# Edge stage of a graph attention kernel: sums, weights and carry in one matmul stream, loops written out, membership in 32 bits

## Chip, cores and metric

One Trainium2 chip, one core. The metric is the device time in microseconds of one launch. All data are float32 except where bf16 is named.

## The reference, cut to what matters

There are 6250 nodes with 512 features, 8 heads of 64 features, and 100000 edges sorted by their destination `dst`.

```
h     = leaky_relu(layernorm(x) @ W.T + b)                 # N x 512
e     = leaky_relu(e_src[src] + e_dst[dst])                # E x 8, from h
a     = exp(e - m[dst]) / segment_sum(exp(...), dst) * dist
out   = segment_sum(h[src] * a, dst)                       # N x 512
x     = x + out
x     = x + ffn(layernorm(x))                              # small per-row network
```

## The kernel before

Four parts run one after the other. `project` makes h in 49 tiles of 128 nodes and stores rows of 520 numbers (512 values and the 8 source scores) in the HBM table `table_h`. `prepare` works out, for each group of edges, the first destination row (its base), the offsets `rel` from it, and a table `table_shifts` of destination scores in three bf16 parts. `attend_windows` (L647 to L955) is the edge stage, and `finish` (L958) divides by the weights, adds x and runs the network over 13 chunks.

The edge stage goes through 112 groups of 7 tiles of 128 edges. One group's destinations lie within a window of 128 rows. Per group:

- GpSimd issues 7 indirect DMAs (L768), each fetching 128 rows of `table_h`, 260 KB, into `gathered`, three slots deep. It waits for an index copy by ACT (`set_src`, L910) and for the messages of the group three before.
- The Vector engine writes the membership matrix in bf16 (L778: does edge p belong to row c). ACT widens it to 32 bits (`widen_member`, L928), TensorE transposes it in bf16 (L873), and ACT copies the transpose back (`turn_member`, L934).
- TensorE looks up the destination scores of each edge: 7 matmuls of 48 columns (`at_edges`, L864). The Vector engine sums the three parts (L786), makes the scores (L790 to L798), and ACT takes the exponentials (L920).
- ACT and the Vector engine split the exponentials into three bf16 parts. The Vector engine makes 7 messages of 512 columns (L810) from `gathered` into `msg`.
- TensorE sums the messages by membership: 7 matmuls 128x512 in float32 (L886, each issued as two instructions), and the weights by 7 bf16 matmuls of 24 columns (L893). ACT copies the sums out (`evacuate`), the Vector engine adds up the weights (L831).
- The last row of one window can be the first of the next. So SP stores a window to `table_agg` (L741), reads one row back for the next group (L752), and the Vector engine adds it (`carry_in`, L841), four rounds behind the front of the pipeline.

The order on each engine is written out by hand: each engine walks through rounds, and `stage(u, slot, lag, do)` lets it do the step `do` for group u - lag. The rounds are a loop of three at a time with register arithmetic (`rounds`, L703). On the Vector engine a round is: carry of u-4, scores of u-1, membership of u, messages of u-1, weights of u-3. On TensorE: lookup of u-1, first three tiles of u-2, transposes of u, the rest of u-2. Engines wait for one another by semaphores that count finished groups; SP's three DMAs of a round are issued in order: window of u, carry of u-4, store of u-4.

## Time and profile before

| what | value |
|---|---|
| time, median of 3 runs (lowest, highest) | 2029.5 us (2019.91 to 2036.35) |
| the profiled execution's own time | 2030.48 us |
| its span in the trace | 2028.7 us |
| TensorE matmul busy | 1406.5 us, 69% |
| Vector engine busy | 1337.0 us, 66% |
| GpSimd busy | 986.9 us, 49% |
| ACT busy | 496.3 us, 24% |
| DMA packets of the gathers | 208.78 MB, 37.1% of 16 engines' span |

The trace begins at the first instruction; starts are in microseconds from there. PE is TensorE's matmul unit, PEld its weight load, DVE the Vector engine, ACT ScalarE, POOL GpSimd, SP the engine that issues plain DMAs. A row's bracket holds the idle time of that engine just before it, and what ended that time; "remote" is a semaphore update for which the trace shows no instruction or DMA close enough in time.

### The profile page before, as it was taken

What the parts mean: (1) busy time and instruction counts of PE and PEld (TensorE: products, weight loads), DVE (VectorE), ACT (ScalarE), POOL (GpSimd) and SP (SyncE); (2) the same over time, 40 slices, a digit from 0 to 9 for tenths busy, and PEclk for the clock granted to TensorE, in tenths of its full rate; (3) what the DMA queues carried; (4) which work ended last, traced back from release to release, by engine and by line L of the source; (5) the groups of instructions that cost most, each with busy time, mean ns of one, the idle gap of its engine ahead of it and who ended that gap; (6) DMA issues with size and microseconds to landing.
All of it is one profiled execution on the core that took longest, in us unless ns stands there. A gap on an engine that the chain in (4) does not pass through costs nothing. (4 is left out here: it accounts for less than half of the span.)

```text
span 2028.7 us, 24635 instructions
## 1 busy us (share of the span) xinstructions
PE 1406.5 (69%) x5502; PEld 662.8 (33%) x5502; DVE 1337.0 (66%) x3092; ACT 496.3 (24%) x1141; POOL 986.9 (49%) x932
## 2 busy tenths in 40 slices
PE   5778783477666676566767676766657665299997
PEld 2333331233232233232323232323223332155555
DVE  5777776467566576665766576666657655868784
ACT  1222220222222222222322222222222221123332
POOL 1222221666656566575556755666666651213231
PEclk9999987688888898888888888888889878578888
DMA  5333333666665566575566765666666653424331
GB/s 216 131 124 126 125 125 64 166 195 191 176 175 172 169 191 191 168 200 168 160 172 194 199 171 159 191 178 174 172 188 182 188 165 91 176 89 167 145 135 67
DMA packets 151399, 326.44 MB, mean 161 GB/s; under 512 B 47312, under 2 KB 47568, under 8 KB 151246
## 3 DMA queue, kind: packets, MB, share of 16 engines
q0 software_dynamic: 62720, 208.78, 37.1%
q1 hardware_dynamic: 88654, 117.38, 17.2%
q8 instruction: 9, 0.15, 0.0%
q14 instruction: 16, 0.13, 0.0%
HBM read 255.82 MB, written 70.27 MB: 161 GB/s over the span
## 5 line engine op out<-in xcount | busy, mean ns | idle before, releaser
L768 POOL DMA_INDIRECT gathered<-table_h,w_src_idx x784 | 827.5, 1055 | 517.2 <-issue 244.3
L886 PE MATMUL bank<-w_msg,member 128*128 128x512 f32 x1568 | 810.3, 662 | 0.0
L810 DVE TENSOR_TENSOR w_msg<-gathered,w_coef 128x512 f32<-128x512 f32 x784 | 489.8, 694 | 3.9
L886 PEld LDWEIGHTS bank<-w_msg,member 128*128 128x128 f32 x1568 | 313.8, 213 | 316.3 <-issue 282.2
L873 PE MATMUL bank<-ident,member 128*128 128x128 bf16 x784 | 72.0, 240 | 313.8 <-DVE member L778 221.2
L786 DVE TENSOR_REDUCE at_dst<-bank 128x112 f32<-128x336 f32 x112 | 56.3, 503 | 326.8 <-remote 259.5
L277 PE MATMUL bank<-wt,xnT 128*128 128x512 f32 x392 | 203.0, 666 | 0.0
L208 POOL TENSOR_TENSOR prod_dst<-hrow,w_dst 128x512 f32<-128x512 f32 x49 | 75.6, 1543 | 250.4 <-DVE hrow L237 250.4
L920 ACT ACTIVATE w_ex<-w_diff 128x56 f32<-128x56 f32 x112 | 27.9, 249 | 673.2 <-issue 348.0
L873 PEld LDWEIGHTS bank<-ident,member 128*128 128x128 bf16 x784 | 53.5, 108 | 402.6 <-DVE member L778 221.4
L1197 PE MATMUL bank<-h,w 128*128 128x512 f32 (+1 forms) x338 | 180.3, 682 | 0.0
L841 DVE TENSOR_TENSOR summed<-summed,w_carry 1x520 f32<-1x520 f32 x111 | 76.4, 688 | 155.7 <-ACT summed L908 126.4
L1114 POOL TENSOR_TENSOR res<-x_in,y 128x2048 f32<-128x2048 f32 (+1 forms) x13 | 61.9, 4765 | 234.9 <-DMA out<-res 162.8
L908 ACT ACTIVATE memberT<-bank 128x896 bf16<-128x896 bf16 x112 | 102.1, 911 | 266.0 <-remote 239.3
L778 DVE TENSOR_TENSOR member<-node_no,k_rel 128x896 bf16<-128x896 f32 x112 | 122.1, 1090 | 9.6 <-DMA node_no<-in_node_no 9.6
L908 ACT ACTIVATE member<-member 128x896 f32<-128x896 bf16 x112 | 106.5, 951 | 64.0 <-issue 35.0
L864 PE MATMUL bank<-window,memberT 128*128 128x48 bf16 x784 | 40.3, 190 | 117.4 <-ACT memberT L908 94.8
L277 PEld LDWEIGHTS bank<-wt,xnT 128*128 128x128 f32 x392 | 78.0, 209 | 95.7 <-issue 95.7
L1197 PEld LDWEIGHTS bank<-h,w 128*128 128x128 f32 x338 | 68.8, 223 | 64.3 <-issue 62.3
L286 PE MATMUL bank<-ident,xn 128*128 128x128 f32 x196 | 32.3, 289 | 78.7 <-DVE xn L227 78.7
L1143 ACT ACTIVATE h<-bank,b 128x512 f32<-128x512 f32 (+1 forms) x65 | 41.7, 661 | 162.7 <-PE bank L1208 90.6
L1208 PEld LDWEIGHTS bank<-w,h 128*128 128x128 f32 x490 | 72.0, 225 | 21.7 <-issue 20.9
(133 smaller groups left out, 1185.8 us busy)
## 6 DMA issues: line engine op xcount, KB each, us to landing
table_agg<-summed SPq DMA_DIRECT2D x112, 260.0 KB
table_agg<-zeros SPq DMA_DIRECT2D x50, 260.0 KB, 2.2
table_h<-hrow SPq DMA_DIRECT2D x49, 260.0 KB, 2.1
xt<-in_x SPq DMA_DIRECT2D x49, 256.0 KB, 2.7
gathered<-table_h,w_src_idx POOLq DMA_INDIRECT x784
agg_in<-table_agg SPq DMA_DIRECT2D x12, 1040.0 KB, 7.7
x_in<-in_x SPq DMA_DIRECT2D x12, 1024.0 KB, 5.4
out<-res SPq DMA_DIRECT2D x12, 1024.0 KB, 4.4
```

The lines of the kernel that those rows point to most:

```text
L208: nc.gpsimd.tensor_tensor(prod_dst[:, s, :], hrow[:, s, 0:D], w_dst[:, :], ALU.mult).then_inc(s_pdst, 1)
L277: mm = nc.tensor.matmul(ps_h[s][:, :], xnT[:, s, c * P:(c + 1) * P], wt[:, c, :], start=False, stop=(c == DC - 1))
L768: pool.indirect_dma_start(out=gathered[:, s, j, :], out_offset=None, in_=t["h"][:, :], in_offset=bass.IndirectOffsetOnAxis(ap=src_idx[:, s ...
L778: nc.vector.tensor_tensor(member16[:, s, :, :], node_no[:, :].unsqueeze(1).to_broadcast([P, GROUP, P]), keep["rel"][:, bass.ds(g * GROUP, ...
L810: nc.vector.tensor_tensor(msg[:, s, j, :].rearrange("p (h d) -> p h d", h=HEADS), gathered[:, s, j, 0:D].rearrange("p (h d) -> p h d", h=H ...
L841: nc.vector.tensor_tensor(summed[0:1, s, :], summed[0:1, s, :], carry[:, :], ALU.add).then_inc(d["carried"], 1)
L873: last = nc.tensor.transpose(member_t[:, j * P:(j + 1) * P], member16[:, s, j, :], ident16[:, :])
L886: nc.tensor.matmul(sums[s][:, :], member[:, s, j, :], msg[:, s, j, :], start=first, stop=final)
L908: return nc.scalar.activation(out, in_, ACT.Copy)
L1114: nc.gpsimd.tensor_tensor(res[:, s, 0:k, :], x[:, s, 0:k, :], y[:, s, 0:k, :], ALU.add).then_inc(d["res"], 1)
L1197: last = nc.tensor.matmul(bank[:, 0:w], w2[:, weights, :], h1[:, units, 0:w], start=(i == 0), stop=(i == len(pairs) - 1))
L1208: last = nc.tensor.matmul(y3[:, 8 * j:8 * j + 8], h2[:, g, j * P:(j + 1) * P], w3[:, g, :], start=(g == 0), stop=(g == 4))
```

## The change

- A row of the tables is now two halves of 260: 256 values and 4 head scores or weights each. Helper functions give the views.
- A group holds 895 edges; the slot of row 32 of its first tile is kept free (`CARRY_ROW`), with offset 0. There are still 112 groups.
- The exponentials are written by ACT into `gathered` itself, beside the values; the messages overwrite the values in place. TensorE sums values and weights together in two matmuls of 260 columns per tile, into two PSUM banks. The separate bf16 weight matmuls, the splitting into parts and the weights' evacuation are gone.
- The carried row is no longer added by the Vector engine. SP reads it from `table_agg` into row 32 of the group's first tile (`carry_in`), and that tile is summed last (`add_rest`). A group's final matmuls thus wait until the group before has been summed, copied out, stored and read back.
- The Vector engine writes the membership in 32 bits; it is transposed in 32 bits over two PSUM banks, and ACT copies it to bf16. ACT's widening is gone.
- The coefficients and the row of node numbers lie in PSUM. The lookup stays in one PSUM bank.
- Four slots in place of three. All loops of the stage are written out, and GpSimd reads its indices from the resident array; ACT's index copy is gone. GpSimd waits for the sums of the group four before.
- DMA semaphores count 16 per transfer in place of 48.
- SP's order in a round: window of u+2, store of u-1, carry of u.

The other parts follow the new row layout. Left out below are removed lines of the edge stage and edits of the same kind elsewhere.

```diff
@@ -30,9 +30,12 @@
 ROWS = NODES + P
 NOWHERE = NODES
 DC = D // P
-ROW = D + HEADS
+HALF = D // 2 + HEADS // 2
+ROW = 2 * HALF
 GROUP = 7
-GROUPS = -(-E // (P * GROUP))
+CARRY_ROW = 32
+GROUP_EDGES = P * GROUP - 1
+GROUPS = -(-E // GROUP_EDGES)
 EDGE_TILES = GROUPS * GROUP
 TINY = 1e-30
 FAR = 1 << 20
@@ -54,6 +57,42 @@
+def row_values(rows):
+    return rows.rearrange("p (a w) -> p a w", a=2)[:, :, 0:D // 2].rearrange("p a (h d) -> p a h d", d=HD)
+def row_heads(rows):
+    return rows.rearrange("p (a w) -> p a w", a=2)[:, :, D // 2:HALF]
+def rows_heads(rows):
+    return rows.rearrange("p k (a w) -> p k a w", a=2)[:, :, :, D // 2:HALF]
+def by_half(heads):
+    return heads.rearrange("p (a h) -> p a h", a=2)
+def tiles_by_half(heads):
+    return heads.rearrange("p k (a h) -> p k a h", a=2)
+def wide(values):
+    return values.rearrange("p (a h d) -> p a h d", a=2, d=HD)
...
                 dve.wait_ge(d["dstf"], 1)
                 step(nc.vector.tensor_tensor(rel, rel, keep["bases"][:, :].unsqueeze(2)
                                                     .to_broadcast(group_dst), ALU.subtract))
+                step(nc.vector.memset(rel[CARRY_ROW:CARRY_ROW + 1, :, 0], 0.0))
                 nc.vector.tensor_reduce(spread[:, 0:GROUPS], rel, AX, ALU.max).then_inc(d["rel_max"], 1)
...
-def attend_windows(nc, top, banks, t, keep, branch_semaphores):
...
+def attend_windows(nc, top, psum, t, keep, branch_semaphores):
     with ExitStack() as ctx:
         def sb(name, shape, dt=F32):
@@ -659,300 +693,237 @@
             return branch_semaphores.pop() if branch_semaphores else top.enter_context(nc.semaphore(name))
...
+        S = 4
+        PARTS = 6 * HEADS
+        gathered = sb("gathered", [P, S, GROUP, ROW])
+        member = sb("member", [P, S, GROUP, P])
+        memberT = sb("memberT", [P, S, GROUP, P], BF16)
+        window = sb("window", [P, S, PARTS], BF16)
         at_dst = sb("at_dst", [P, GROUP, 2 * HEADS])
         score = sb("w_score", [P, GROUP, HEADS])
         leaky = sb("w_leaky", [P, GROUP, HEADS])
...
+        diff = sb("w_diff", [P, S, GROUP, HEADS])
+        summed = sb("summed", [P, S, ROW])
+        node_sb = sb("node_no", [P, P])
+        member_t = psum[:, 4:6, :].rearrange("p b c -> p (b c)")
+        coef = psum[:, 6, 0:GROUP * HEADS]
+        node_no = psum[:, 6, GROUP * HEADS:GROUP * HEADS + P]
+        s_no, s_no_kept = sem("node_no_loaded"), sem("node_no_kept")
         s_pool_on = sem("w_pool_went_on")
...
+        s_g = [sem(f"w_gathered{i}") for i in range(S)]
+        s_put = [sem(f"w_stored{i}") for i in range(S)]
+        s_carry = sem("w_carry_put")
+        s_win = [sem(f"w_window_loaded{i}") for i in range(S)]
+        names = ("member member_t memberT edge_dst at_dst score leaky diff ex coef msg sums evac").split()
         d = {k: sem("w_" + k) for k in names}
...
+        def filled(g, per):
+            return per * (g // S + 1)
+        def sums_of(slot):
+            return psum[:, 2 * (slot % 2):2 * (slot % 2) + 2, 0:HALF]
+        def edge_dst(slot):
+            return psum[:, 7, 0:GROUP * PARTS]
+        def rounds(lead, drain):
+            for u in range(-lead, GROUPS + drain):
+                yield u, u % S
         def stage(u, slot, lag, do):
...
+            if not 0 <= u - lag < GROUPS:
                 return
...
+            do(u - lag, (slot - lag) % S)
+        def old(g, slots=S):
+            return g >= slots
         with nc.Block() as block:
             @block.sync
             def _(sp):
...
+                sp.dma_start(node_sb[:, :], t["node_no"]).then_inc(s_no, 16)
+                def base_of(g):
+                    return sp.value_load(keep["bases_int"][0:1, g:g + 1], min_val=0, max_val=NODES)
                 def load_window(g, s):
...
+                    base = base_of(g)
                     if old(g):
...
+                        sp.wait_ge(d["edge_dst"], g - S + 1)
+                    sp.dma_start(window[:, s, :], t["shifts"][bass.ds(base, P), :]).then_inc(s_win[s], 16)
                 def store(g, s):
...
+                    base = base_of(g)
+                    if old(g, 1):
+                        before = (s - 1) % S
+                        sp.wait_ge(s_put[before], filled(g - 1, 16))
+                    sp.wait_ge(d["evac"], g + 1)
+                    sp.dma_start(t["agg"][bass.ds(base, P), :], summed[:, s, :]).then_inc(s_put[s], 16)
+                def carry_in(g, s):
+                    to = gathered[CARRY_ROW:CARRY_ROW + 1, s, 0, :]
+                    if not old(g, 1):
+                        sp.wait_ge(d["msg"], 1)
+                        sp.dma_start(to, t["h"][NODES:NODES + 1, :]).then_inc(s_carry, 16)
                         return
...
+                    base = base_of(g)
+                    before = (s - 1) % S
+                    sp.wait_ge(s_put[before], filled(g - 1, 16))
+                    sp.wait_ge(d["msg"], g * GROUP + 1)
+                    sp.dma_start(to, t["agg"][bass.ds(base, 1), :]).then_inc(s_carry, 16)
+                for u, slot in rounds(2, 1):
+                    stage(u, slot, -2, load_window)
+                    stage(u, slot, 1, store)
+                    stage(u, slot, 0, carry_in)
+                for g in range(GROUPS - S, GROUPS):
+                    sp.wait_ge(s_put[g % S], filled(g, 16))
             @block.gpsimd
             def _(pool):
...
+                for g in range(GROUPS):
+                    s = g % S
                     if old(g):
...
+                        wait_alone(pool, d["sums"], g - S + 1, s_pool_on)
                     for j in range(GROUP):
                         pool.indirect_dma_start(
                             out=gathered[:, s, j, :], out_offset=None, in_=t["h"][:, :],
...
+                            in_offset=bass.IndirectOffsetOnAxis(ap=keep["src"][:, g, j:j + 1], axis=0)
+                        ).then_inc(s_g[s], 16)
             @block.vector
             def _(dve):
                 def make_member(g, s):
                     if old(g):
...
+                        dve.wait_ge(d["sums"], g - S + 1)
                     nc.vector.tensor_tensor(
...
+                        member[:, s, :, :], node_no.unsqueeze(1).to_broadcast([P, GROUP, P]),
+                        keep["rel"][:, g * GROUP:(g + 1) * GROUP].unsqueeze(2).to_broadcast([P, GROUP, P]),
+                        ALU.is_equal).then_inc(d["member"], 1)
                 def scores(g, s):
...
                     dve.wait_ge(d["edge_dst"], g + 1)
                     nc.vector.tensor_reduce(
...
+                        at_dst[:, :, :], edge_dst(s).rearrange("p (j q c) -> p j c q", j=GROUP, q=3), AX, ALU.add
+                    ).then_inc(d["at_dst"], 1)
                     dve.wait_ge(d["at_dst"], g + 1)
...
+                    dve.wait_ge(s_g[s], filled(g, 16 * GROUP))
+                    nc.vector.tensor_tensor(tiles_by_half(score[:, :, :]), rows_heads(gathered[:, s, :, :]),
+                                            tiles_by_half(at_dst[:, :, 0:HEADS]), ALU.add).then_inc(d["score"], 1)
                     dve.wait_ge(d["score"], g + 1)
                     nc.vector.scalar_tensor_tensor(leaky[:, :, :], score[:, :, :], SLOPE, score[:, :, :], ALU.mult,
                                                    ALU.max).then_inc(d["leaky"], 1)
                     dve.wait_ge(d["leaky"], g + 1)
                     if old(g):
...
+                        dve.wait_ge(d["ex"], g - S + 1)
                     nc.vector.tensor_tensor(diff[:, s, :, :], leaky[:, :, :], at_dst[:, :, HEADS:], ALU.subtract
                                             ).then_inc(d["diff"], 1)
                 def messages(g, s):
                     dve.wait_ge(d["ex"], g + 1)
...
+                    nc.vector.tensor_tensor(
+                        tiles_by_half(coef.rearrange("p (j h) -> p j h", j=GROUP)), rows_heads(gathered[:, s, :, :]),
+                        tiles_by_half(keep["dist"][:, g * GROUP:(g + 1) * GROUP, :]), ALU.mult
+                    ).then_inc(d["coef"], 1)
                     dve.wait_ge(d["coef"], g + 1)
...
                     for j in range(GROUP):
+                        values = row_values(gathered[:, s, j, :])
                         nc.vector.tensor_tensor(
...
+                            values, values, by_half(coef[:, j * HEADS:(j + 1) * HEADS]).unsqueeze(3)
+                            .to_broadcast([P, 2, HEADS // 2, HD]), ALU.mult).then_inc(d["msg"], 1)
                 dve.wait_ge(s_no, 16)
...
+                nc.vector.tensor_copy(node_no, node_sb[:, :]).then_inc(s_no_kept, 1)
+                dve.wait_ge(s_no_kept, 1)
+                for u, slot in rounds(1, 0):
+                    stage(u, slot, 0, scores)
+                    stage(u, slot, -1, make_member)
+                    stage(u, slot, 0, messages)
             @block.tensor
             def _(pe):
+                def transpose(g, s):
+                    pe.wait_ge(d["member"], g + 1)
+                    if old(g, 1):
+                        pe.wait_ge(d["memberT"], g)
+                    for j in range(GROUP):
+                        last = nc.tensor.transpose(member_t[:, j * P:(j + 1) * P], member[:, s, j, :],
+                                                   keep["ident"][:, :])
+                    last.then_inc(d["member_t"], 1)
                 def at_edges(g, s):
...
                     pe.wait_ge(d["memberT"], g + 1)
...
+                    pe.wait_ge(s_win[s], filled(g, 16))
+                    if old(g, 1):
                         pe.wait_ge(d["at_dst"], g)
                     for j in range(GROUP):
...
+                        last = nc.tensor.matmul(edge_dst(s)[:, j * PARTS:(j + 1) * PARTS], memberT[:, s, j, :],
                                                 window[:, s, :], start=True, stop=True)
                     last.then_inc(d["edge_dst"], 1)
...
+                def add_tile(g, s, j, start, stop):
+                    for a in range(2):
+                        last = nc.tensor.matmul(sums_of(s)[:, a, :], member[:, s, j, :],
+                                                gathered[:, s, j, a * HALF:(a + 1) * HALF], start=start, stop=stop)
+                    return last
+                def add_first(g, s):
+                    pe.wait_ge(d["member"], g + 1)
+                    if old(g, 2):
+                        pe.wait_ge(d["evac"], g - 1)
+                    for j in range(1, 5):
                         pe.wait_ge(d["msg"], g * GROUP + j + 1)
...
+                        add_tile(g, s, j, j == 1, False)
+                def add_rest(g, s):
+                    for j in range(5, GROUP):
+                        pe.wait_ge(d["msg"], g * GROUP + j + 1)
+                        add_tile(g, s, j, False, False)
+                    pe.wait_ge(s_carry, 16 * (g + 1))
+                    add_tile(g, s, 0, False, True).then_inc(d["sums"], 1)
+                for u, slot in rounds(1, 0):
+                    stage(u, slot, -1, transpose)
+                    stage(u, slot, 0, add_first)
+                    stage(u, slot, -1, at_edges)
+                    stage(u, slot, 0, add_rest)
             @block.scalar
             def _(act):
                 def copy(out, in_):
                     return nc.scalar.activation(out, in_, ACT.Copy)
...
                 def exps(g, s):
                     act.wait_ge(d["diff"], g + 1)
...
+                    nc.scalar.activation(rows_heads(gathered[:, s, :, :]), tiles_by_half(diff[:, s, :, :]), ACT.Exp
+                                         ).then_inc(d["ex"], 1)
                 def turn_member(g, s):
                     act.wait_ge(d["member_t"], g + 1)
                     if old(g):
...
+                        act.wait_ge(d["edge_dst"], g - S + 1)
                     copy(memberT[:, s, :, :], member_t[:, 0:GROUP * P].rearrange("p (j c) -> p j c", j=GROUP)
                          ).then_inc(d["memberT"], 1)
                 def evacuate(g, s):
                     act.wait_ge(d["sums"], g + 1)
                     if old(g):
...
+                        act.wait_ge(s_put[s], filled(g - S, 16))
+                    copy(summed[:, s, :].rearrange("p (a w) -> p a w", a=2), sums_of(s)).then_inc(d["evac"], 1)
+                for u, slot in rounds(1, 1):
+                    stage(u, slot, 0, exps)
+                    stage(u, slot, 1, evacuate)
+                    stage(u, slot, -1, turn_member)
...
-                    nc.vector.tensor_scalar_max(wsum[:, 0:k, :], ak[:, :, D:ROW], TINY).then_inc(d["wsum"], 1)
+                    nc.vector.tensor_scalar_max(tiles_by_half(wsum[:, 0:k, :]), rows_heads(ak), TINY).then_inc(d["wsum"], 1)
...
-        banks = [top.enter_context(nc.psum_tensor(f"bank{i}", [P, 512], F32)) for i in range(8)]
+        psum = top.enter_context(nc.psum_tensor("bank", [P, 8, 512], F32))
+        banks = [psum[:, i, :] for i in range(8)]
...
+    edge_slots = np.delete(np.arange(GROUP * P), CARRY_ROW)
     for name, ends in (("src", src), ("dst", dst)):
-        padded = np.full(EDGE_TILES * P, NOWHERE, np.int32)
+        padded = np.full(GROUPS * GROUP_EDGES, NOWHERE, np.int32)
         padded[:E] = ends
-        a[name] = padded.reshape(GROUPS, GROUP, P).transpose(2, 0, 1)
+        slots = np.full((GROUPS, GROUP * P), NOWHERE, np.int32)
+        slots[:, edge_slots] = padded.reshape(GROUPS, GROUP_EDGES)
+        a[name] = slots.reshape(GROUPS, GROUP, P).transpose(2, 0, 1)
```

## Rows read from the trace of the kernel before

**Rows 1.** Windows: length; busy PE, PEld, DVE, ACT, POOL; PEclk, DMA share, GB/s
```profile
356.00:1724.00 1368.00, 902.70 (x3920) 412.37 (x3920) 862.32 (x1903) 343.30 (x783) 827.45 (x784) 0.85 0.62 176
1724.00:2028.70 304.70, 258.39 (x945) 145.79 (x945) 223.00 (x706) 82.16 (x158) 81.56 (x91) 0.79 0.36 130
```

**Rows 2.** Line L768: ns least/median/greatest, first and last start
```profile
L768 POOL DMA_INDIRECT gathered<-table_h,w_src_idx x784: 940/946/1869, 356.8 to 1683.6; - x196
```

**Rows 3.** Groups by line, 356:1724: busy, mean ns | idle before, its end
```profile
L768 POOL DMA_INDIRECT gathered<-table_h,w_src_idx x784 | 827.5, 1055 | 517.2 <-issue 244.3 <-DVE w_msg L810 149.0 <-ACT w_src_idx L908 123.9
L886 PE MATMUL bank<-w_msg,member 128*128 128x512 f32 x1568 | 810.3, 662 | 0.0
L810 DVE TENSOR_TENSOR w_msg<-gathered,w_coef 128x512 f32<-128x512 f32 x784 | 489.8, 694 | 3.9
...
L908 ACT ACTIVATE member<-member 128x896 f32<-128x896 bf16 x112 | 106.5, 951 | 64.0 <-issue 35.0 <-DVE member L778 29.0
L841 DVE TENSOR_TENSOR summed<-summed,w_carry 1x520 f32<-1x520 f32 x111 | 76.4, 688 | 155.7 <-ACT summed L908 126.4 <-issue 11.6 <-DVE summed L831 10.0
...
L908 ACT ACTIVATE summed<-bank 128x512 f32<-128x512 f32 x112 | 66.2, 591 | 10.0 <-PE bank L893 10.0
L786 DVE TENSOR_REDUCE at_dst<-bank 128x112 f32<-128x336 f32 x112 | 56.3, 503 | 326.8 <-remote 259.5 <-PE bank L864 55.6 <-DMA gathered<-table_h,w_src_idx 11.6
```

**Rows 4.** Timeline from 909 us, a short round: start, duration, engine, line
```profile
909.83 0.51 DVE L786 TENSOR_REDUCE at_dst<-bank 128x112 f32<-128x336 f32 x1 [7.18 <-remote]
...
911.00 1.08 DVE L778 TENSOR_TENSOR member<-node_no,k_rel 128x896 bf16<-128x896 f32 x1
911.28 1.63 POOL L768 DMA_INDIRECT gathered<-table_h,w_src_idx  x1 [0.30 <-issue]
...
912.38 4.30 DVE L810 TENSOR_TENSOR w_msg<-gathered,w_coef 128x512 f32<-128x512 f32 x7
```

**Rows 5.** Timeline 918 to 947 us: a lookup's end and who waits for it
```profile
918.18 0.51 DVE L786 TENSOR_REDUCE at_dst<-bank 128x112 f32<-128x336 f32 x1 [0.32 <-PE bank L864]
...
926.18 0.34 PE L864 MATMUL bank<-window,memberT 128*128 128x48 bf16 x7 [0.38 <-issue]
...
934.47 0.95 POOL L768 DMA_INDIRECT gathered<-table_h,w_src_idx  x1 [0.30 <-issue]
938.37 0.51 DVE L786 TENSOR_REDUCE at_dst<-bank 128x112 f32<-128x336 f32 x1 [10.04 <-remote]
...
946.13 1.10 POOL L768 DMA_INDIRECT gathered<-table_h,w_src_idx  x1 [10.72 <-DVE w_msg L810]
```

**Rows 6.** Groups by line, `project`: a Vector operation with one PSUM input
```profile
L237 DVE TENSOR_TENSOR hrow<-leak,bank 128x512 f32<-128x512 f32 x43 | 29.4, 683 | 22.3 <-ACT leak L305 21.2
```

**Rows 7.** Timeline of PE: summing, and 32-bit transposes of `project`
```profile
152.53 0.65 PE L286 MATMUL bank<-ident,xn 128*128 128x128 f32 x4 [0.99 <-DVE xn L227]
...
1700.43 6.25 PE L886 MATMUL bank<-w_msg,member 128*128 128x512 f32 x14
```

**Rows 8.** The same pair after the last gather, 1713 to 1719 us
```profile
1713.48 0.42 SPq L741 DMA_DIRECT2D table_agg<-summed  x1
1715.76 0.28 SPq L752 DMA_DIRECT2D w_carry<-table_agg  x1
1717.21 0.69 DVE L841 TENSOR_TENSOR summed<-summed,w_carry 1x520 f32<-1x520 f32 x1 [2.87 <-DMA w_carry<-table_agg]
1718.07 0.42 SPq L741 DMA_DIRECT2D table_agg<-summed  x1
```

**Rows 9.** SP's stores and carry loads while gathers run, 902 to 928 us
```profile
902.83 0.43 SPq L741 DMA_DIRECT2D table_agg<-summed  x1
...
907.09 0.56 SPq L752 DMA_DIRECT2D w_carry<-table_agg  x1
918.03 0.42 SPq L741 DMA_DIRECT2D table_agg<-summed  x1
...
927.51 0.70 SPq L752 DMA_DIRECT2D w_carry<-table_agg  x1
```

251 lines of the change are left out of this document (32 added, 219 removed).

## The prediction

> **What bounds the kernel now.** I read the windows of the parts first. The edge stage takes 1368.0 of the span of 2028.7 us [rows 1], and in it no engine is busy all the time: TensorE 66%, the Vector engine 63%, GpSimd 60%, DMA at a share of 0.62. `finish` is left as it is but for views. So the question is what a round of the edge stage waits for. The first and the last of the 784 gathers start at 356.8 and 1683.6 us [rows 2], which makes a round of 7 gathers 7 x 1326.8 / 783 = 11.86 us, and 1368 - 112 x 11.86 = 40 us for the last group's way through.
>
> Next the groups by line [rows 3]. GpSimd spends a median of 946 ns on a gather [rows 2], and 0.30 us stand ahead of each one, also where it waits for nothing [rows 4, 5]: 1.25 us, or 8.75 us a round. Its waits beyond that are named: 149.0 us for messages and 123.9 us for the index copy. GpSimd is held back, so it is not the bound. The Vector engine waits 326.8 us ahead of the sum of the looked-up parts (L786), and 155.7 us ahead of the carry (L841).
>
> The timeline shows how. A short round is 918.18 - 909.83 = 8.35 us from one L786 to the next [rows 4, 5]; the Vector engine is then almost never idle. In the long round that follows, the lookup's matmuls are over at 926.5 us, and the Vector engine starts on them only at 938.37 us [rows 5], 11.9 us later, released by something that the view calls remote. GpSimd was issuing gathers all that time, the last at 934.47; then it stood until 946.13, since its slots were full. I read this as TensorE's announcement arriving late while gathers run. It is the reading that my number rests on most: 326.8 / 112 = 2.92 us a round. And 8.35 + 2.92 = 11.27, with 0.6 left to 11.86 for carry and order.
>
> **The change, part by part.** *Short round, Vector engine.* Gone are the carry add (688 ns [rows 3]), two splits (about 0.2 us each) and the weights' sum (about 0.2 us). Messages stay at 7, each with one input in PSUM now; such an operation of 512 columns takes 683 ns in `project` [rows 6], against 694 [rows 3], so no change. The membership in 32 bits: 896 columns in 1.08 us with bf16 out [rows 4]. 32 bits out can't be shorter than that by much (a 1x pass, as 896 columns against the messages' 512 show) and could cost more; I bound it by 1.08 and twice that, and take 1.1, since the rows with 32-bit output have the same time per column. That leaves about 7.1 us a round.
>
> *Short round, TensorE.* Seven tiles of 512 columns take 6.25 us [rows 7]; 520 columns in two matmuls instead of one are 6.25 x 520/512 = 6.35, if a weight load stays hidden behind 260 columns. If it doesn't, the bound is twice as many loads of 213 ns, their mean, beside matmuls: 14 x 0.2 = 2.8 us more. I take the first, as a 512 column matmul repeats every 0.43 us and a load is half of it. Transposes in 32 bits: four take 0.65 us in `project` [rows 7], seven about 1.0, where bf16 takes 0.93 at the low clock. The lookup is 0.34 us [rows 5], the weight matmuls (about 0.33 us) go. Together 7.7 us a round, a little more than before. In sequence: first message over 3.24 us after L786 (2.55 to its start, then 0.69 [rows 4]), tile 1 a message later at 3.85, four tiles of 0.91 us until 7.5, lookup until 7.8, next L786 at 7.9. A short round is 7.9 us, set by TensorE instead of the Vector engine.
>
> *GpSimd.* A gather beside a busy Vector engine is stretched, to 1.63 us at 911.28 us under the membership [rows 4], while it is 0.95 in the idle stretch [rows 5]. The mean is 1055 ns against a median of 946: 784 x 0.109 = 85 us. Node numbers and coefficients in PSUM may take this away. It is worth nothing as long as GpSimd waits for slots, and is kept for a rival below. The index copy's 123.9 us go too, and what is late next is the free slot. That is now given by the sums of four groups ago instead of the messages of three; sums trail messages by some 4 us, so GpSimd gains about half a round of lead.
>
> The Trainium skill, page SBUF — State Buffer, section Who interferes with whom, says that a Vector instruction with two SBUF inputs blocks GpSimd's reads only, and infers that descriptor generation isn't held up by it. By that the PSUM placing gives nothing and the 85 us stay; the stretched gather at 911.28 speaks against it.
>
> *ACT.* Its widening (951 ns), two small copies and the index copy go, the evacuation grows by 8 columns. ACT is busy a quarter of the stage; zero either way, covered by waits.
>
> *Late announcements.* Three a round come from TensorE, as before: transposes, lookup, sums. I keep 2.92 us a round; below it lies zero, above it twice the value, as the sums' announcement is now inside the carry's loop.
>
> *The carry's loop.* Before, it ran four rounds behind. Now each group's last matmuls wait for it, and behind them in TensorE's queue stand the next group's transposes, tiles and lookup. One turn of the loop: store issue to carry landed, then the last tile (0.91 plus 0.2 us), the copy out (591 ns [rows 3]) and 0.2 us of hand-overs, so 1.9 us. Without gathers, store to carry is 1717.21 - 1713.48 = 3.73 us [rows 8]. With gathers it is 907.09 - 902.83 = 4.26 to the issue [rows 9], and 1.45 to land [rows 8], so 5.7; in the slow stretch 9.48 + 1.45 = 10.9 [rows 9], where SP itself was slow. The turn is 5.6, 7.6 or 12.8 us. At 7.6 it is hidden under a round of 10.8; 0.1 us a round is what I put on it, from the 12.8 us turns that fall together with long rounds anyway.
>
> *The rest.* One more Vector step in `prepare`, below 1 us. Loops written out: the register work between instructions goes, which no row puts on a path; nothing.
>
> *Sum.* 7.9 + 2.9 + 0.1 = 10.9 us a round; 112 x 10.9 + 40 = 1261 us against 1368, so 107 us less. The profiled execution took 2030.5 us (span 2028.7), 1 us over the median of 2029.5. That gives 1923, rounded to 1920 us.
>
> **The rivals.**
> *A. GpSimd's rate becomes the bound.* If late announcements go away with this rewrite (the fourth slot, increments of 16, fewer engines waiting), a round is 8.75 us: 1020 us for the stage, a time of about 1680. With the stretched gathers it is 7 x 1.355 = 9.49, and 1770. For it: GpSimd was the next in line by 2 us a round. Against: nothing in the diff touches the gathers' traffic, beside which lateness appears. Chance 0.21.
> *B. Announcements come only when the gathers pause.* After the last gather at 934.47 + 0.95 the lookup was taken up 2.95 us later [rows 5]. If a round always needs such a pause, it is 8.75 + 2.95 = 11.7 us whatever the other engines save: 1351 us, about 2013, within 1%. With smaller variations of other terms, chance 0.13.
> *C. The carry's loop stops TensorE; slower.* Place: the wait for the carry ahead of the last tile. Price: the middle of the 7.6 and 12.8 us turns, 10.2, plus one late announcement of 2.92 that the loop now holds, makes 13.1 us a round; 1508 us, a time of 2170. It decides from 11.86 us a turn up. For it: SP needed 9.5 us from store to carry load in a stretch with gathers [rows 9], and GpSimd will run gathers more of the time. Against: the short turn of 7.6 leaves 3 us. Chance 0.26, mostly between 2050 and 2180.
> That the change doesn't do what it says I take as no case: the operations are plainly other ones.
>
> **How the numbers follow.** The forecast's own case, 1790 to 2005 us (short rounds of 7.9 to 8.7 with 2 to 3 us of lateness), has 0.40. About 1% is what a measurement of this kernel can tell from no change, 20 us. Faster by over 1%: 0.40 + 0.21 = 0.61. Within: 0.13. Slower: 0.26. The range goes from 1690, which leaves out 0.07 below (A without a rest), to 2130, which leaves out about 0.11 of C.
>
> **What would show it.** Right: the mean distance of two gather groups falls from 11.86 to about 10.9 us; L786's counterpart still waits for "remote" or TensorE some 300 us in all; the Vector engine's share falls below 60%; matmuls of 260 columns repeat every 0.22 us. A shows as gathers 1.25 us apart without gaps and a mean of 0.95 us. B shows as a pause of about 3 us after each 7 or 14 gathers. C shows as TensorE idle ahead of its last tile, released by the carry's DMA, and gathers held by sums. Wrong in size would be weight loads that no longer hide (matmuls of 260 columns over 0.3 us apart), and a membership of 2 us.

## The result, and the profile after

The changed kernel takes 1934.7 us (median of 4 runs, 1919.3 to 1954.7) where the kernel before takes 2024.7; the ratio is 0.956, 95% interval 0.945 to 0.967. The forecast was 1920 us. Medians are of all executions, ratios of those in which the chip was not slowed by a lower granted clock, so a ratio can differ from the quotient of two medians. The profiled execution took 1919.3 us with a span of 1917.7, 110.9 us less than the span before.

Windows of the kernel after (columns as in [rows 1]): first the edge stage, then everything from TensorE's first instruction of `finish` on.

```profile
356.00:1635.00 1279.00, 943.29 (x4704) 756.06 (x4704) 736.42 (x1457) 191.09 (x337) 741.21 (x784) 0.89 0.66 189
1665.60:1917.70 252.10, 234.65 (x945) 133.68 (x945) 200.54 (x658) 80.60 (x155) 77.88 (x85) 0.90 0.37 136
```

The same second window before, from its own first instruction of `finish`:

```profile
1753.10:2028.70 275.60, 258.39 (x945) 145.75 (x945) 200.49 (x658) 80.36 (x155) 76.10 (x86) 0.82 0.34 125
```

So 23.5 of the 110.9 us are hardly the change's: `finish` has the same matmuls, and TensorE was busy in it for 23.7 us less at a granted clock of 0.90 instead of 0.82. The stretch from first to last gather went from 1326.8 us [rows 2] to 1248.0 (next row), 78.8 less. The last 8.6 us lie between the two.

The gathers' line after (as [rows 2]), and the groups by line of 356 to 1635 us (as [rows 3]):

```profile
L797 POOL DMA_INDIRECT gathered<-table_h,k_src x784: 940/946/1297, 356.7 to 1604.7; - x196
```

```profile
L875 PE MATMUL bank<-gathered,member 128*128 128x260 f32 x3136 | 817.6, 416 | 61.8 <-DVE gathered L839 39.8 <-issue 14.0 <-DMA gathered<-table_agg 7.7
L797 POOL DMA_INDIRECT gathered<-table_h,k_src x784 | 741.2, 945 | 524.8 <-issue 237.0 <-PE bank L875 169.6 <-remote 118.2
...
L839 DVE TENSOR_TENSOR gathered<-gathered,bank 128x512 f32<-128x512 f32 x784 | 478.7, 683 | 3.8
...
L807 DVE TENSOR_TENSOR member<-bank,k_rel 128x896 f32<-128x896 f32 x112 | 121.4, 1084 | 0.1
...
L903 ACT ACTIVATE summed<-bank 128x520 f32<-128x520 f32 x112 | 66.5, 594 | 71.8 <-remote 45.0 <-PE bank L875 14.8 <-issue 12.0
L814 DVE TENSOR_REDUCE at_dst<-bank 128x112 f32<-128x336 f32 x112 | 56.9, 508 | 510.9 <-remote 401.3 <-PE bank L868 108.5 <-issue 1.1
```

A round is 7 x 1248.0 / 783 = 11.16 us, where 10.9 was forecast. One gather of 784 takes over 1 us, 1297 ns, where 228 did before (mean 945 ns, before 1055). The Vector engine is busy 736 of 1279 us (58%), and nearly all its idle time stands ahead of L814, which answers to L786: 511 us, 4.56 a round.

The timeline of a regular round after:

```profile
904.26 0.94 POOL L797 DMA_INDIRECT gathered<-table_h,k_src  x1 [4.13 <-PE bank L875]
...
909.20 0.34 PE L868 MATMUL bank<-window,memberT 128*128 128x48 bf16 x7
...
909.38 2.88 PE L875 MATMUL bank<-gathered,member 128*128 128x260 f32 x12
...
911.76 0.95 POOL L797 DMA_INDIRECT gathered<-table_h,k_src  x1 [0.30 <-issue]
912.84 0.51 DVE L814 TENSOR_REDUCE at_dst<-bank 128x112 f32<-128x336 f32 x1 [4.38 <-remote]
...
914.35 0.60 ACT L903 ACTIVATE summed<-bank 128x520 f32<-128x520 f32 x1
...
915.13 0.94 POOL L797 DMA_INDIRECT gathered<-table_h,k_src  x1 [2.42 <-remote]
915.15 0.75 PEld L858 LDWEIGHTS bank<-ident,member 128*128 128x128 f32 x7 [3.31 <-DVE member L807]
915.15 0.98 PE L858 MATMUL bank<-ident,member 128*128 128x128 f32 x7 [2.90 <-DVE member L807]
915.17 0.35 SPq L769 DMA_DIRECT2D table_agg<-summed  x1
```

Seven gathers run from 904.26 to 912.71. The lookup is over at 909.54, and the Vector engine takes it up at 912.84, 0.13 us after the last gather's end. The sums are over at 912.26; ACT takes them at 914.35, and GpSimd starts the next run at 915.13. That is rival B's picture: a run of 8.45 us, a pause of 2.4 us, in which the announcements arrive. Set against the trace's record of every semaphore, it holds widely. Of 112 lookups 92 end inside a run; 96 are announced over 0.3 us late, and 88 of those 96 only outside a run. Early in a run it is different: 61 of the 112 announcements of transposes fall due 1 to 3 us into one, and their median delay is 0.01 us, while 52 lookups fall due 5 to 7 us into one and are 3.0 us late on average. Only TensorE's announcements are late. Those on record of the Vector engine's and ACT's once-a-round operations in this stage all come within 0.5 us of the operation's end (median 0.01), in both kernels.

### The profile page after: what moved, and what is told of

Same layout as the page of the kernel before. It is cut to its first block and busy times, and to the rows that moved or that the text cites. A ratio compares the mean times of both kernels' runs of the same rounds, so it can differ in the third digit from the quotient of the medians.

```text
span 1917.7 us, 22261 instructions
## 1 busy us (share of the span) xinstructions
PE 1422.5 (74%) x6286; PEld 994.0 (52%) x6286; DVE 1211.4 (63%) x2647; ACT 343.9 (18%) x692; POOL 902.5 (47%) x932
## 5 line engine op out<-in xcount | busy, mean ns | idle before, releaser
L797 POOL DMA_INDIRECT gathered<-table_h,k_src x784 | 741.2, 945 | 524.8 <-issue 237.0
L875 PE MATMUL bank<-gathered,member 128*128 128x260 f32 x3136 | 817.6, 416 | 61.8 <-DVE gathered L839 39.8
L875 PEld LDWEIGHTS bank<-gathered,member 128*128 128x128 f32 x3136 | 627.7, 207 | 188.2 <-issue 79.4
L839 DVE TENSOR_TENSOR gathered<-gathered,bank 128x512 f32<-128x512 f32 x784 | 478.7, 683 | 3.8
L814 DVE TENSOR_REDUCE at_dst<-bank 128x112 f32<-128x336 f32 x112 | 56.9, 508 | 510.9 <-remote 401.3
L858 PE MATMUL bank<-ident,member 128*128 128x128 f32 x784 | 130.4, 315 | 290.4 <-DVE member L807 274.1
L858 PEld LDWEIGHTS bank<-ident,member 128*128 128x128 f32 x784 | 100.7, 160 | 333.0 <-DVE member L807 313.6
L903 ACT ACTIVATE memberT<-bank 128x896 bf16<-128x896 f32 x112 | 102.6, 916 | 181.4 <-PE bank L858 108.6
L807 DVE TENSOR_TENSOR member<-bank,k_rel 128x896 f32<-128x896 f32 x112 | 121.4, 1084 | 0.1
L903 ACT ACTIVATE summed<-bank 128x520 f32<-128x520 f32 x112 | 66.5, 594 | 71.8 <-remote 45.0
L1179 PE MATMUL bank<-w,h 128*128 128x8 f32 x490 | 62.6, 262 | 0.5 <-ACT h L1114 0.5
```

What stands on the lines that cost most here:

```text
L797: pool.indirect_dma_start(out=gathered[:, s, j, :], out_offset=None, in_=t["h"][:, :], in_offset=bass.IndirectOffsetOnAxis(ap=keep["src"][ ...
L807: nc.vector.tensor_tensor(member[:, s, :, :], node_no.unsqueeze(1).to_broadcast([P, GROUP, P]), keep["rel"][:, g * GROUP:(g + 1) * GROUP]. ...
L814: nc.vector.tensor_reduce(at_dst[:, :, :], edge_dst(s).rearrange("p (j q c) -> p j c q", j=GROUP, q=3), AX, ALU.add).then_inc(d["at_dst"], 1)
L839: nc.vector.tensor_tensor(values, values, by_half(coef[:, j * HEADS:(j + 1) * HEADS]).unsqueeze(3) .to_broadcast([P, 2, HEADS // 2, HD]), ...
L858: last = nc.tensor.transpose(member_t[:, j * P:(j + 1) * P], member[:, s, j, :], keep["ident"][:, :])
L875: last = nc.tensor.matmul(sums_of(s)[:, a, :], member[:, s, j, :], gathered[:, s, j, a * HALF:(a + 1) * HALF], start=start, stop=stop)
```

## The experiments

Each ratio is to the kernel before, timed beside the experiment on the same chip. Experiments 1 to 4, 5 to 8, 9 to 11 and 12 ran on four chips, and the kernel after was not timed again on them. So its 0.956 is compared across chips, and small differences to it prove little.

Two theories were put against each other. S is the sum of the prediction: work of a short round plus late announcements. L (later L2) says that an unbroken run of gathers holds back what TensorE announces, until the run ends. To compare kernels I split each round into the gathers, 7 x (mean + 0.30 us), and the rest, in which GpSimd stands. Before that is 9.48 + 2.38 = 11.86 us [rows 2, 3], after 8.72 + 2.44 = 11.16.

**1. After, with the PSUM placing undone.**

```diff
-        coef = psum[:, 6, 0:GROUP * HEADS]
-        node_no = psum[:, 6, GROUP * HEADS:GROUP * HEADS + P]
+        coef = sb("w_coef", [P, GROUP * HEADS])[:, :]
+        node_no = sb("node_no_kept", [P, P])[:, :]
```

> The changed kernel with coefficients and node numbers back in SBUF, nothing else. Theory L (a round is one run of 7 gathers plus a pause of 2.4 us, because TensorE's announcements that fall due inside a run come only at its end): the gathers are stretched again, mean 1.05 instead of 0.945 us, so a run is 0.77 us longer and the time rises by 112 x 0.77 = 86 us, to about 2020 us; the gain over the kernel before is gone. Theory S (the prediction's sum: a round is TensorE's short round of 7.9 us plus 2.9 us of late announcements, and GpSimd waits for slots anyway): the gathers are stretched, but the time stays at 1935 us within 1%.

1891.6 us, ratio to before 0.948 (0.939 to 0.958). Its gathers' line, and two groups by line:

```profile
L797 POOL DMA_INDIRECT gathered<-table_h,k_src x784: 940/946/1897, 358.8 to 1576.3; - x196
```

```profile
L797 POOL DMA_INDIRECT gathered<-table_h,k_src x784 | 793.4, 1012 | 442.1 <-issue 241.2 <-PE bank L875 103.1 <-remote 97.8
...
L814 DVE TENSOR_REDUCE at_dst<-bank 128x112 f32<-128x336 f32 x112 | 56.9, 508 | 467.8 <-remote 334.4 <-PE bank L868 108.8 <-issue 24.7
```

The gathers are stretched again, and the time does not rise: 9.18 + 1.70 = 10.88 us a round. Theory L as written falls here. Against this run the kernel after has shorter gathers (8.72) and longer pauses (2.44), so the placing brought nothing that can be seen. The hold is weaker here: 29 lookups fall due 5 to 7 us into a run, and half of them are announced within 0.02 us, where the median of the 52 in the kernel after is 3.1 us.

**2. Before, with that placing alone.**

```diff
-        node_no = sb("node_no", [P, P])
+        node_sb = sb("node_no", [P, P])
+        node_no = banks[5][:, 0:P]
...
-        coef = sb("w_coef", [P, GROUP, HEADS])
+        coef = banks[7][:, 0:GROUP * HEADS].rearrange("p (j h) -> p j h", j=GROUP)
```

> The kernel before, with only its coefficients and node numbers put in two free PSUM banks. Theory L: the gathers' mean falls from 1.055 to 0.945 us, and the time by up to 86 us, to 1940 to 1960 us, with nothing else of the rewrite done. Theory S: gathers shorter, time 2025 us within 1%, as the round is set by the Vector engine's work plus late announcements.

2163.6 us, ratio 1.088 (1.077 to 1.099): slower, which neither theory expected. Its gathers' line and the timeline of one lookup:

```profile
L769 POOL DMA_INDIRECT gathered<-table_h,w_src_idx x784: 942/949/1337, 356.0 to 1832.9; - x196
```

```profile
935.10 0.33 PE L867 MATMUL bank<-window,memberT 128*128 128x48 bf16 x7
...
944.45 0.94 POOL L769 DMA_INDIRECT gathered<-table_h,w_src_idx  x1 [0.30 <-issue]
947.98 0.51 DVE L787 TENSOR_REDUCE at_dst<-bank 128x112 f32<-128x336 f32 x1 [12.24 <-remote]
...
955.63 1.11 POOL L769 DMA_INDIRECT gathered<-table_h,w_src_idx  x1 [10.24 <-DVE w_msg L811]
```

A round is 8.81 + 4.39 = 13.20 us. Here 14 gathers run without a break, 0.95 us each, and the lookup that was over at 935.43 is taken up 12.6 us later, 2.6 us after the run's end. The hold is as long as what is left of the run. The unbroken runs got no longer on average: counting gathers under 0.4 us apart as one run, there are 79 runs of 9.9 gathers, where the kernel before has 58 of 13.5. What rose is the lookups' mean delay, from 2.6 to 4.9 us. Where Vector operations stretch the gathers, announcements do get through inside a run (experiment 1). That this is why taking the stretching away costs more than it brings is argued from the two runs, not shown.

**3. After, with the lookup a round ahead.**

```diff
-                for u, slot in rounds(1, 0):
-                    stage(u, slot, -1, transpose)
+                for u, slot in rounds(2, 0):
+                    stage(u, slot, -1, at_edges)
+                    stage(u, slot, -2, transpose)
                     stage(u, slot, 0, add_first)
-                    stage(u, slot, -1, at_edges)
                     stage(u, slot, 0, add_rest)
```

(The membership and ACT's copy of it move a round ahead likewise.)

> The changed kernel with membership, transposes and lookup one round further ahead: the lookup of group g+1 stands at the head of TensorE's round g instead of in its middle, so its announcement has a whole round to arrive. Theory L: the Vector engine no longer stands at the end of each run; its idle time ahead of the sum of looked-up parts falls from 511 us to under 150, and the round becomes the gathers' own 8.75 us if TensorE's sums can be announced late without stopping GpSimd: 1935 - 112 x 2.2 = 1690 us; if each run still needs its pause for the sums, 1900 to 1935. Theory S: TensorE's own sequence stays, lateness leaves the path: 7.9 to 8.75 us a round, the same 1690. A rival H, that lateness is TensorE being behind its modelled times and not held announcements: no change, 1935 us.

1865.0 us, ratio 0.937 (0.926 to 0.948, which overlaps after's interval at its edge); 8.72 + 1.89 = 10.61 us a round. Timeline and group by line:

```profile
910.41 0.34 PE L868 MATMUL bank<-window,memberT 128*128 128x48 bf16 x7
910.59 0.96 PE L858 MATMUL bank<-ident,member 128*128 128x128 f32 x7
911.39 5.21 PE L875 MATMUL bank<-gathered,member 128*128 128x260 f32 x23
...
921.12 0.95 POOL L797 DMA_INDIRECT gathered<-table_h,k_src  x1 [0.30 <-issue]
...
924.66 0.92 ACT L903 ACTIVATE memberT<-bank 128x896 bf16<-128x896 f32 x1 [12.12 <-remote]
```

```profile
L903 ACT ACTIVATE memberT<-bank 128x896 bf16<-128x896 f32 x112 | 102.6, 916 | 482.4 <-remote 373.5 <-PE bank L858 84.9 <-issue 24.0
...
L814 DVE TENSOR_REDUCE at_dst<-bank 128x112 f32<-128x336 f32 x112 | 56.2, 502 | 219.2 <-remote 205.1 <-PE bank L868 8.8 <-issue 5.4
```

The Vector engine's wait fell by 292 us, but the round by only 0.55: the expected 1690 us failed. The lateness moved to the transposes. They are over at 911.55, ACT gets them at 924.66, 2.6 us after a run of 14 gathers ends, and in ACT's queue the exponentials stand behind them. TensorE itself went on with its sums at 911.39, so its work was not late, only its word.

**4. After, with an eighth of the bytes.**

```diff
-                            out=gathered[:, s, j, :], out_offset=None, in_=t["h"][:, :],
+                            out=gathered[:, s, j, :] if g < S else gathered[:, s, j, 0:65], out_offset=None,
+                            in_=t["h"][:, :] if g < S else t["h"].rearrange("r (b c) -> (r b) c", b=8),
```

> The changed kernel with gathers that bring 65 columns (260 bytes) a row instead of 520, from the fifth group on; it leaves out the rest of each row and reads other rows, the number of gathers and descriptors stays. If announcements are held by GpSimd issuing gathers: runs of 8.5 us remain, announcements still come at their ends, time 1935 us within 1.5%. If they are held by the gathers' traffic: the Vector engine's idle time ahead of the sum of looked-up parts goes from 511 to under 150 us, the round falls to 8 to 8.8 us and the time to 1610 to 1700 us.

1908.7 us (one run), beside 2000.3 for the kernel before on the same chip; the window of its edge stage and its gathers' line:

```profile
356.00:1600.00 1244.00, 926.15 (x4696) 745.31 (x4697) 736.03 (x1457) 191.34 (x336) 740.19 (x784) 0.90 0.23 52
```

```profile
L797 POOL DMA_INDIRECT gathered<-table_h,k_src x784: 938/944/1297, 355.9 to 1577.1; - x196
```

DMA moves 52 GB/s instead of 189, and a round is still 8.71 + 2.21 = 10.92 us. So the bytes moved are not what holds the announcements. What is left is GpSimd's issuing itself, or the DMA queue's handling of the row requests, whose number this run keeps; no run separates the two.

**5. After, with GpSimd waiting for the lookup ahead of its 5th gather.**

```diff
                     for j in range(GROUP):
+                        if old(g) and j == 4:
+                            wait_alone(pool, d["edge_dst"], g - 1, s_pool_on)
```

> The changed kernel with one more wait in GpSimd's queue: ahead of the 5th of its 7 gathers it waits for the lookup that TensorE does meanwhile, so that a run is cut where that announcement falls due. Theory L2 (GpSimd's issuing holds back what TensorE announces later than some 3 us into an unbroken run, until the run ends): the lookup's announcement comes within 1 us of its end, the Vector engine's idle time ahead of the sum of looked-up parts falls from 511 to under 250 us, and the round from 11.1 to 9 to 9.8 us: 1700 to 1800 us. Rival T (lateness belongs to TensorE's own queue, or to the number of gathers under way, and not to the unbroken run): the added wait only delays gathers; no change or slower, 1935 to 2050 us.

1882.9 us, ratio 0.945 (0.938 to 0.953): far from the 1700 to 1800 expected. The timeline:

```profile
910.76 0.95 POOL L799 DMA_INDIRECT gathered<-table_h,k_src  x1 [0.30 <-issue]
910.99 0.34 PE L870 MATMUL bank<-window,memberT 128*128 128x48 bf16 x7
...
913.17 0.51 DVE L816 TENSOR_REDUCE at_dst<-bank 128x112 f32<-128x336 f32 x1 [3.98 <-remote]
...
913.94 0.94 POOL L799 DMA_INDIRECT gathered<-table_h,k_src  x1 [2.24 <-remote]
```

The run was not cut, it was shifted: of 109 restarts after a pause 108 now stand ahead of a 5th gather, and 106 of 111 runs are still 7 gathers long. Each lookup is announced 1.5 us after a run's end (median), and none of the 105 late ones inside a run. So the hold follows the run wherever the run is put, which speaks for L2 and against T. L2's price was wrong, since a pause costs 2.3 us each time.

**6. Experiment 3 with a wait for the transposes ahead of the 4th gather.**

```diff
+                        if old(g) and j == 3:
+                            wait_alone(pool, d["member_t"], g, s_pool_on)
```

> The version with membership, transposes and lookup a round ahead, and a wait ahead of GpSimd's 4th gather of a group for the transposes that TensorE does meanwhile. Theory L2: a long run can no longer form while TensorE owes an announcement; the transposes' late announcements (ACT idle 373 us by remote) go below 100 us, the round falls from 10.6 to 8.9 to 9.5 us, 1865 us to 1660 to 1740. Rival T: as the added wait costs GpSimd time, 1865 us or more.

1845.3 us, ratio 0.927 (0.919 to 0.935); 8.72 + 1.78 = 10.50 us a round. The ratio is lower than in experiment 3, but the intervals overlap. The size expected by L2 failed: 40 pauses stand ahead of a first gather and 34 ahead of a 4th, so one kind of pause took the place of another.

**7. After, with the 32-bit membership undone** (Vector engine writes bf16, TensorE transposes bf16, ACT widens):

```diff
-                        member[:, s, :, :], node_no.unsqueeze(1).to_broadcast([P, GROUP, P]),
+                        member16[:, s, :, :], node_no.unsqueeze(1).to_broadcast([P, GROUP, P]),
...
+                    copy(member[:, s, :, :], member16[:, s, :, :]).then_inc(d["member"], 1)
```

> The changed kernel with the membership part undone: written in bf16 by the Vector engine, transposed in bf16 by TensorE, widened to 32 bits by ACT. Theory S and theory L2 alike: ACT's 0.95 us a round beside the transposes is covered, transposes cost 0.9 to 1.0 us either way: 1915 to 1950 us, no change. A rival for it (32 bits on the Vector engine save a hand-over from ACT on the path): slower by 112 x 0.5 to 1 us, 1990 to 2050 us.

1920.0 us, ratio 0.962 (0.954 to 0.970), where after has 0.956: no difference that can be told. The part that names the change brought nothing.

**8. Before, with its loop written out and no index copy.**

```diff
-                    wait_alone(pool, s_idx, g + 1, s_pool_on)
...
-                            in_offset=bass.IndirectOffsetOnAxis(ap=src_idx[:, s, j:j + 1], axis=0)
+                            in_offset=bass.IndirectOffsetOnAxis(ap=keep["src"][:, g, j:j + 1], axis=0)
```

> The kernel before with its edge stage's loop written out and the gathers' indices read where they lie, so without ACT's index copy and GpSimd's 124 us of waits for it; nothing else of the rewrite. Theory S (GpSimd is held back by slots anyway; register work is on no path): 2025 us within 1%. Theory L2: GpSimd waits for messages instead, at longer unbroken runs, so announcements are no earlier: 2025 to 2100 us. Rival R (the gain came with the written-out loops and the missing index copy): 1920 to 1960 us.

2087.3 us against 1988.5, ratio 1.039 (1.026 to 1.052). Three things changed at once: the loops, ACT's index copy and GpSimd's wait of 124 us for it. Together they made the kernel slower. So rival R falls, and letting GpSimd run on did not help, as in experiment 2. Which of the three costs the time was not tried.

**9 and 10. Both kernels with gathers in their first groups alone.**

> The changed kernel with gathers for its first 4 groups alone; later groups compute on what then lies in the slots, so its outputs are not the reference's. It measures a round without gathers. Theory S as written in the prediction: the short round is 7.9 us, set by TensorE. Theory L2 the same, and all idle time of the Vector engine ahead of the sum of looked-up parts that is called remote (401 us) goes, since nothing is issued that could hold an announcement: stage of about 900 us, time of about 1555 us. If TensorE's lateness were its own (its matmuls really taking longer than modelled), the round would stay at 10 to 11 us.

> The kernel before with gathers for its first 3 groups alone; later groups compute on what then lies in the slots, so its outputs are not the reference's. Its short round by the prediction is 8.35 us: 112 x 8.35 = 935 us for the stage, time of about 1620 us. By theory L2 no lookup is announced late any more (the Vector engine's 260 us by remote go). The difference to the changed kernel without gathers is what the rewrite saved in work and order: 0.45 us a round if theory S's terms hold.

1557.8 and 1579.8 us (one run each). The line of the looked-up sums, after and then before, and after's group by line:

```profile
L814 DVE TENSOR_REDUCE at_dst<-bank x112: 507/507/508, 358.8 to 1255.1; 128x112 f32<-128x336 f32 x112
```

```profile
L786 DVE TENSOR_REDUCE at_dst<-bank x112: 487/489/509, 368.8 to 1262.9; 128x112 f32<-128x336 f32 x112
```

```profile
L814 DVE TENSOR_REDUCE at_dst<-bank 128x112 f32<-128x336 f32 x112 | 56.8, 507 | 149.0 <-PE bank L868 127.4 <-remote 21.6
```

First to last, that is 896.3 / 111 = 8.07 us a round after and 894.1 / 111 = 8.05 before. But these means hold the start. The second and third of these sums, after and then before:

```profile
393.80 0.51 DVE L814 TENSOR_REDUCE at_dst<-bank 128x112 f32<-128x336 f32 x1 [21.60 <-remote]
403.25 0.51 DVE L814 TENSOR_REDUCE at_dst<-bank 128x112 f32<-128x336 f32 x1 [2.74 <-PE bank L868]
```

```profile
380.48 0.51 DVE L786 TENSOR_REDUCE at_dst<-bank 128x112 f32<-128x336 f32 x1 [4.58 <-issue]
389.37 0.51 DVE L786 TENSOR_REDUCE at_dst<-bank 128x112 f32<-128x336 f32 x1 [1.90 <-PE bank L864]
```

The kernel after issues its first 28 gathers in one run, also here, and its second lookup is taken up only behind it, 35.0 us after the first; before, that step is 11.7 us. From the third sum to the last a steady round is (1255.1 - 403.25) / 109 = 7.82 us after and (1262.9 - 389.37) / 109 = 8.01 before. Two things follow. The 401 us of "remote" are gone but for that one wait of 21.6 us, so all lateness comes with the gathers. And the rewrite's saved operations are worth 0.19 us a round by themselves, which the slower start eats up here. Of the 22 us between the two times, 10 lie ahead of the first lookup (358.8 against 368.8) and 8 in `finish`.

The Trainium skill, page Perfetto Trace Analysis, section Summary: the profiler window per engine type, says that TensorE's end in the profile is estimated and the propagation of its semaphore hidden, so that lateness could be work still going on. Here it isn't: with no gathers the same matmuls are announced on time, and in experiment 3 TensorE's next matmuls are recorded while the word is still out.

**11. Experiment 3 with the PSUM placing undone.**

> The version with membership, transposes and lookup a round ahead, with coefficients and node numbers back in SBUF. Theory L2 with what e1_sbuf showed (gathers stretched under Vector operations with two SBUF inputs let announcements through inside a run): the gathers cost 0.4 us a round more, the pauses 0.7 us less: ratio to before 0.925 to 0.935, where the same version with them in PSUM had 0.937. Theory S: nothing, 0.937. A rival (stretched gathers add to a round that they set now): 0.955.

1846.0 us, ratio 0.9215 (0.914 to 0.929): faster than the kernel before, and its interval lies below after's, which was measured on another chip. A round is 9.25 + 1.29 = 10.54 us.

```profile
L797 POOL DMA_INDIRECT gathered<-table_h,k_src x784: 940/946/1867, 355.8 to 1534.7; - x196
```

As L2 expected, gathers are 0.5 us a round longer than in experiment 3 and pauses 0.6 shorter.

**12. Lookup ahead, GpSimd's wait of experiment 6 and no PSUM placing, together.**

> The version a round ahead with coefficients and node numbers in SBUF, and GpSimd's wait ahead of the 4th gather of a group for TensorE's transposes. Theory L2, if the two effects add: runs of 14 gathers (43 of 58 in e11_ahead_sbuf) are cut, ACT's idle time by remote ahead of the turned membership goes from 223 to under 120 us: ratio to before 0.905 to 0.918. A rival (each cut run costs its own pause of 2.3 us, and that eats what earlier announcements bring): 0.92 to 0.93.

1723.2 us, ratio 0.957 (0.952 to 0.961). This ran on another chip. There the kernel before took 1803.9 us, where it had taken 1988.5 to 2024.7 elsewhere, and its granted clock was 0.93 where it had been 0.86. The ratio can't be set beside the others, and the question of the run stays open. Its gathers' line and the longest waits:

```profile
L799 POOL DMA_INDIRECT gathered<-table_h,k_src x784: 942/947/2066, 358.3 to 1410.0; - x196
```

```profile
DVE w_score L821 <- DMA gathered<-table_h,k_src: 307.6, 112, 7.6
POOL gathered L799 <- issue: 253.1, 776, 16.8
```

On that chip all 784 gathers run without a pause, 7 x 1051.7 / 783 = 9.40 us a round, and the 224 announcements of transposes and sums arrive within 0.02 us of their ends. Rival A, which put 9.49 us on a round of stretched gathers, is what bounds it. No other kernel was traced on this chip, so the trace does not tell whether the chip or the kernel's version ended the hold; that the kernel before gained 10% there too speaks for the chip.

## Why the prediction was right

**The time.** 1920 forecast, 1934.7 measured; by profiled executions 1923 and 1919.3, helped by 23.5 us in `finish`, at a higher clock, that I had not put in. In the stage alone 107 us were forecast and 87 came (78.8 + 8.6). So the close hit is in part luck.

**Terms that held.** Membership in 32 bits 1084 ns (1.1 us put), messages 683, seven transposes 0.98 us (1.0), copy out 594, the Vector engine's share 58% (below 60%). From L814 to the lookup's end it was 7.78 us at the full clock (923.74 to 931.52), with 7.8 put. Matmuls of 260 columns repeat every 2.88 / 12 = 0.24 us (0.22 put), weight loads stay hidden. The clock was my gap: in the round from 912.84 us that stretch was 9.16 us long, and 16 matmuls in it took 5.13 us instead of 3.75. The windows of those matmuls show a granted clock of 0.73, a mean of both levels, and of 1.00:

```profile
916.70:921.80 5.10, 5.10 (x22) 4.14 (x23) 2.84 (x5) 0.39 (x1) 3.88 (x5) 0.73 0.77 210
927.60:931.30 3.70, 3.70 (x21) 3.14 (x22) 2.85 (x5) 0.40 (x1) 2.78 (x4) 1.00 0.75 197
```


**Late announcements.** I kept this term as it was, and by the lookups' own delay it stayed: 2.61 us on average from end to announcement before, 2.75 after. The 2.92 that I wrote was another measure, all idle time ahead of the sum of looked-up parts, with 67 us of waits for TensorE and DMA in it. By that measure the term grew to 4.56 us a round, and the sign of "some 300 us in all" came out at 511, 401 of them remote against 259.5 [rows 3]: the Vector engine has less to do (busy 736 us, before 862 [rows 1]) and waits the longer. Nor is the delay a constant that a rewrite leaves alone, as I treated it. It is what is left of a run when the word falls due: 3.3 us in after's regular round, 11.9 us before [rows 5], 12.6 in experiment 2. Rival B named that mechanism, at 0.13, and its sign is there: 92 of 111 runs are 7 gathers long, with a pause behind each. It had the price too high: 2.95 us of pause in each round, where the mean is 2.44.

**A step that was wrong.** The short round of 7.9 us, set by TensorE, holds: it is 7.82 without gathers, and each sum of looked-up parts then waits 1.1 us for TensorE. What failed is the 8.35 that it was set against. That was one round, read while gathers ran; without gathers the kernel before has 8.01. So the work saved is 0.19 us a round, and not 0.45. The other 0.5 us of the forecast gain, the rest "for carry and order" falling from 0.6 to 0.1, had no row that showed where the 0.6 went. With gathers a round can be taken from the third of these sums to the last. The third, before and after:

```profile
398.54 0.51 DVE L786 TENSOR_REDUCE at_dst<-bank 128x112 f32<-128x336 f32 x1 [9.90 <-PE bank L864]
```

```profile
407.22 0.51 DVE L814 TENSOR_REDUCE at_dst<-bank 128x112 f32<-128x336 f32 x1 [4.18 <-PE bank L868]
```

The last start at 1700.7 and 1619.9 us, so a round is 11.95 us before and 11.13 after. Of the 0.82 gained, 0.63 is in what the gathers add to a round: 3.94 us before, 3.31 after. The lower clock is in these too, 0.85 before and 0.89 after from 356 us to the last gather, against 0.99 and 0.98 without gathers. And the start costs the kernel after 17 us (46.4 us from the first sum to the third, 29.6 before): its second lookup is taken up only 35.5 us after the first, behind an unbroken run of 28 gathers. That was not forecast either, and took back most of what `finish` gave.

Which part of the rewrite makes the gathers add less is narrowed and not settled. The PSUM placing (1), the 32 bits (7) and the written-out loops with the index copy (8) show no gain by themselves. The fourth slot, messages in place, GpSimd waiting for sums, the carry inside the sums and the order in TensorE's queue were not tried one by one. The delays tell where to look: the transposes' mean delay fell from 2.7 to 0.4 us and the sums' from 2.5 to 1.4, while the lookups' stayed (over the announcements on record, 96 to 112 of each). The number of gathers in an unbroken run does not explain the times by itself. Before had 58 runs of 13.5 on average and after 111 of 7.1, but experiment 2 is the slowest with 79 of 9.9, and experiment 11 is among the fastest with 59 of 13.3.

**Rivals.** A did not come in the kernel after (pauses of 2.44 us a round) and did in experiment 12, on its chip. C is refuted: TensorE's matmuls waited 7.7 us for the carry's DMA in all. The stretched gather of [rows 4] and the Trainium skill (page SBUF — State Buffer, section Who interferes with whom) were on opposite sides: measured, gathers take 1012 ns on average in experiment 1 and 945 with the two operands in PSUM. So the page's inference that descriptor generation isn't held up does not carry over to these gathers. They also read their row numbers from SBUF, and no run tells whether it is these reads that are blocked, which the page would allow. The time did not follow, for another reason than the page's: pauses grew as gathers shrank.

## What to carry to other kernels

When one engine's idle time is named "remote", look at what GpSimd issues meanwhile, and ask of each announcement where in a run of gathers it falls due. Put hand-overs from TensorE a full round ahead of their use (0.956 to 0.937 here, with intervals that overlap, and 0.9215 with the gathers left stretched). Don't expect a freer GpSimd to help while others wait for TensorE's word: in experiments 8 and 2 the kernel before lost 4 and 9%. Measure a round without the gathers first, and leave the first rounds out of the mean: it tells at once what saved operations can pay.

## What was not expected of the hardware

- TensorE's announcements are held while GpSimd issues unstretched gathers back to back. In the kernel after they are on time in the first 3 us of a run (median 0.01 us). Later ones mostly come at its end or up to 2.6 us after it. The Vector engine's and ACT's were not held. Rows of 260 bytes instead of 2080 leave the hold in place (10.92 us a round against 11.16).
- SP's own instructions are slow in the same stretches: the one at 909.18 us took 0.71 us, where the same one took 0.02 at 905.19, early in that run. Of 163 such in the first 4 us of a run one took over 0.3 us, of 135 later ones 47 did.
- Chips differ: on one of those used the unchanged kernel before was 10% faster (1803.9 us, at a granted clock of 0.93), and in the one kernel traced there no announcement was held.
- `finish`, with the same instructions, took 252.1 to 275.6 us, at a granted clock of 0.90 and 0.82.
